# Where the pieces of the next key and value projections stand between weighing and scores, in a two-layer Perceiver kernel

## The reference, cut to what matters

```python
q, k, v = norm(x) @ Wq, context @ Wk, context @ Wv     # keys and values: 4096 x 64 per head
scores = q @ k.T * scale (+ bias)                       # 256 x 4096 per head
out = softmax(scores) @ v                               # then all heads @ Wo, added to x
```

## Time and profile before

| what | value |
|---|---|
| median of 3 runs | 2159.23 us (2150.01 to 2159.76) |
| the profiled execution, its own time | 2159.08 us |
| its span in the profile | 2157.3 us |
| busy: PE, PEld | 1940.9 us (90%), 1322.9 us (61%) |
| busy: DVE, ACT, POOL | 1633.2 (76%), 838.4 (39%), 928.3 (43%) us |
| mean granted TensorE clock | 0.941 of full speed |

### The profile page before, as it was taken

The page is one execution under the profiler, slowest core; times in us unless marked ns, Lnnn a source line. Parts: engine busy times, 40 slices in busy tenths (PEclk is TensorE's granted clock), DMA queues, the critical chain, the costliest instruction groups (busy, mean ns, idle before and its releaser), DMA issues. The chain is left out here.

```text
span 2157.3 us, 34519 instructions
## 1 busy us (share of the span) xinstructions
PE 1940.9 (90%) x12560; PEld 1322.9 (61%) x12562; DVE 1633.2 (76%) x2131; ACT 838.4 (39%) x1108; POOL 928.3 (43%) x438
## 2 busy tenths in 40 slices
PE   8999999999749889899999999999999999997526
PEld 5666666666339778656666666665666666665224
DVE  3566676667596356689988898899988999889572
ACT  3655665656330135223433334333343334334101
POOL 0354655546540034014645456454655446455200
PEclk9999999999868579999999999999999999999758
DMA  2000110000100062000000000110000000000001
GB/s 105 8 13 7 63 32 12 12 7 3 47 0 1 1 244 78 10 8 1 12 12 12 12 0 12 51 51 10 3 12 12 12 1 12 12 8 5 20 0 49
DMA packets 27717, 52.45 MB, mean 24 GB/s; under 512 B 4227, under 2 KB 15252, under 8 KB 27156
## 3 DMA queue, kind: packets, MB, share of 16 engines
q1 hardware_dynamic: 27200, 51.60, 7.4%
q10 hardware_dynamic: 468, 0.16, 0.0%
HBM read 51.23 MB, written 0.52 MB: 24 GB/s over the span
## 5 line engine op out<-in xcount | busy, mean ns | idle before, releaser
L298 POOL TENSOR_TENSOR biased_sums<-biased_sums,biased_scores 128x1024 f32<-128x1024 f32 x218 | 515.2, 2363 | 209.5 <-ACT biased_scores L524 206.1
L573 DVE TENSOR_TENSOR biased_scores<-ps,bias 128x1024 f32<-128x1024 f32 x256 | 311.1, 1215 | 79.6 <-PE ps L369 79.6
L524 ACT ACTIVATE biased_scores<-biased_scores 128x1024 f32<-128x1024 f32 x256 | 268.2, 1053 | 244.6 <-DVE biased_scores L594 243.6
L587 DVE TENSOR_TENSOR ps<-ps,biased_scores 128x512 f32<-128x512 f32 x480 | 331.9, 691 | 3.6
L594 DVE TENSOR_TENSOR biased_scores<-biased_scores,ps 128x1024 f32<-128x1024 f32 x256 | 305.0, 1211 | 11.9 <-PE ps L409 11.9
L298 POOL TENSOR_TENSOR plain_sums<-plain_sums,plain_scores 128x1024 f32<-128x1024 f32 x106 | 250.5, 2363 | 83.9 <-ACT plain_scores L524 74.9
L329 PEld LDWEIGHTS ps<-weights_again,context_again 128*128 128x128 f32 x2048 | 238.2, 192 | 70.7 <-issue 34.0
L329 PE MATMUL ps<-weights_again,context_again 128*128 128x128 f32 x2048 | 262.5, 281 | 13.5 <-ACT biased_keys L497 11.0
L320 PE MATMUL ps<-context_again,weights_again 128*128 128x512 f32 x512 | 253.0, 617 | 19.3 <-ACT biased_values L508 16.7
L369 PE MATMUL ps<-biased_queries,biased_keys 64*128 64x256 f32 x2048 | 257.4, 390 | 6.6 <-DVE biased_scores L573 5.8
L587 DVE TENSOR_TENSOR ps<-ps,plain_scores 128x512 f32<-128x512 f32 x240 | 167.4, 697 | 115.7 <-ACT plain_scores L519 111.4
(11 more groups left out here) (360 smaller groups left out, 2335.9 us busy)
## 6 DMA issues: line engine op xcount, KB each, us to landing
context<-in_ctx_t SPq DMA_DIRECT2D x8, 1024.0 KB, 5.7
moe_w<-in_moe_w SPq DMA_DIRECT2D x32, 256.0 KB, 2.8
context_again<-in_ctx_t SPq DMA_DIRECT2D x8, 1024.0 KB, 6.3
weights_again<-in_wqkv SPq DMA_DIRECT2D x45, 128.0 KB, 2.1
bias<-in_fside SPq DMA_DIRECT2D x1, 4096.0 KB, 22.6
biased_w_out<-in_w_out SPq DMA_DIRECT2D x16, 256.0 KB, 2.7
weights<-in_wqkv SPq DMA_DIRECT2D x21, 128.0 KB, 2.1
plain_w_out<-in_w_out SPq DMA_DIRECT2D x8, 256.0 KB, 2.6
```

The lines of the kernel that those rows point to most:

```text
L298: pool.tensor_tensor(both(SUM[:, :, :, :]), both((E[:, 0] if kp == 1 else SUM)[:, :, :, :]), both(E[:, kp, :, :, :]), ALU.add).then_inc(su ...
L524: act.activation(at, at, ACT.Exp).then_inc(exp_done, 1)
L573: dve.tensor_tensor(E[:, kp, :, :, :].rearrange("p (h t) n j -> p h t (n j)", h=2), scores_bank(kp).rearrange("p (h t n) -> p h t n", h=2, ...
L587: ins = dve.tensor_tensor(to, highest, E[:, kp, :, n, :], ALU.max)
```

## The change

In the two tables every group now has its piece between weighing and scores, and groups 2, 3 and 5, which have two pieces, have the second one after the scores, as they had. So V0, V1, V4, K3 and K4 move from behind the scores of groups 0, 1, 4, 6 and 7 to before them. The order of the pieces among themselves stays. The same loop on ScalarE follows; in the biased stage ScalarE's own order of instructions is the same as before, as it copies no scores there.

```diff
-BEFORE_SCORES = {2: ("V", 2), 3: ("V", 3), 5: ("V", 5)}
-AFTER_SCORES = {0: ("V", 0), 1: ("V", 1), 2: ("K", 0), 3: ("K", 1), 4: ("V", 4), 5: ("K", 2), 6: ("K", 3), 7: ("K", 4)}
+BEFORE_SCORES = {0: ("V", 0), 1: ("V", 1), 2: ("V", 2), 3: ("V", 3), 4: ("V", 4), 5: ("V", 5), 6: ("K", 3), 7: ("K", 4)}
+AFTER_SCORES = {2: ("K", 0), 3: ("K", 1), 5: ("K", 2)}
@@ TensorE
-                            if g in BEFORE_SCORES:
-                                piece(m, BEFORE_SCORES[g])
+                            piece(m, BEFORE_SCORES[g])
                             scores(m + 1, 2 * g)
                             scores(m + 1, 2 * g + 1)
-                            piece(m, AFTER_SCORES[g])
+                            if g in AFTER_SCORES:
+                                piece(m, AFTER_SCORES[g])
@@ ScalarE
-                            if g in BEFORE_SCORES:
-                                piece_out(m, BEFORE_SCORES[g])
+                            piece_out(m, BEFORE_SCORES[g])
                             if not biased:
                                 scores_out(m + 1, 2 * g, attending)
                                 scores_out(m + 1, 2 * g + 1, attending)
-                            piece_out(m, AFTER_SCORES[g])
+                            if g in AFTER_SCORES:
+                                piece_out(m, AFTER_SCORES[g])
```

## The result

The changed kernel takes 2269.8 us (median of 6 runs, 2261.8 to 2275.9), the kernel before 2152.6 us (6 runs with those shown). The ratio is 1.0534, with a 95% interval of 1.0507 to 1.0561: slower, by 117 us, where 80 were forecast and 2260 was the upper end. The profiled execution took 2270.6 us (span 2268.8), against 2159.08, so 111.5 us more; the profiled execution of the kernel before lies 6.5 us above the median of its six runs, so 111.5 and not 117 is the number to hold against the forecast of 80. Beside the first group of experiments one run of the kernel before took 8308.1 us; it is slow, and counts in no ratio.

A forecast was written before the change was run, and what follows sets the result against it. TensorE and VectorE were taken to run nearly in step, tied through ScalarE's in-order queue. Biased loop 73.4, slow loads 2, END - 2 1.8, earlier sweeps -1.4, plain loop 4.2: 80.0 us on 2159.1, so 2239 us, range 2206 to 2260.

The forecast's parts named there:

- Step 1: Sweep start: V0 waits 1.17 us for its weights and starts at 3.05; VectorE's first block comes 3.15 us later.
- Steps 2 to 5: Biased sweep: late VectorE delays K0 and K2, K4 delays the last scores; sweep grows 5.24 us to 73.8.
- step 3: Biased sweep, blocks 6 and 8: block 6 is 3.15 us late, block 8 waits 0.8; K2 starts 3.93 late.
- step 5: Biased sweep's end: V6's 0.69 us wait goes, reciprocal comes at 61.93 against 56.69; the chain behind it is unchanged.
- the clock falls: Rival: added TensorE idle time drops its clock to half, 2.4 us once in each of 14 sweeps; 2273 us, chance 0.06.
- Step 6: Other sweeps: slow first loads cost 2 us in all, biased END - 2 costs 1.8, sweeps before the loops gain 1.4.
- Step 7: Plain loop: V0 waits 1.17 us, the reciprocal comes with the last maximum; 0.7 us per sweep, 4.2 in six.
- TensorE stays the bound: Rival: V6's wait of 0.69 to 0.76 us goes in each of 20 sweeps; faster, 2144 us, chance 0.04.
- Only the load costs: Rival: load waits 1.17 us, V6 gives back 0.76; 0.4 us in 20 sweeps, 2167 us, chance 0.04.
- the load is in time: Rival: V0 starts at 1.88 without waiting, the coupling holds; 1.17 us less per loop sweep, 2214 us, chance 0.12.

The follow-up runs named there:

- order on ScalarE alone: Changed kernel, but in the biased loop ScalarE copies a group's piece out before the second exponential of the group before: 2203.4 us, 1.0229.
- The filled waits: Changed kernel with two filler matmuls before K0 and two before the peaks are spread, in the biased loop and END - 2: 2235.6 us, 1.0371.
- The last version: Kernel before with V6 writing the bank of the lowered peaks and all lowerings two blocks ahead: 2121.0 us, 0.9849.
- the version with both cures: Changed kernel with the value weights' load issued first and all VectorE lowerings two blocks ahead: 2165.7 us, 1.0056.
- the one without V0: Changed kernel with V0 back behind the scores of group 0, the other four pieces still moved: 2208.9 us, 1.0251.
- K3 and K4 alone: Kernel before with only K3 and K4 moved ahead of the scores of groups 6 and 7: 2191.9 us, 1.0171.
- the early load: Changed kernel with the value weights' load issued first in SyncE's turn, ahead of query and key weights: 2244.1 us, 1.0408.
- the two lowerings first in the changed kernel: Changed kernel with VectorE lowering blocks 4 and 5 before the first scores: 2254.0 us, 1.0464.
- V0 alone: Kernel before with only V0 of the five pieces moved before the scores: 2210.5 us, 1.0257.

## Why the prediction was wrong

The direction and the mechanism of the waits held, the size did not: 111.5 us on the profiled executions, with 80 forecast.

*Step 1.* V0's load: 3.05 forecast; in the 14 biased sweeps V0 starts at 2.77 to 3.67 us, in the first at 4.02, on the average of all 0.27 late. Near enough, and in the plain loop right on the average (3.04).

*Steps 2 to 5.* Counted from the weighing at 1192.97: block 6 at 28.13 (27.83 forecast), block 14 at 56.57 (56.26), the reciprocal at 62.24 (61.93), the spreading of the peaks at 66.91 (66.61). Each is 0.3 late by the load. This is a sweep whose clock held up to its end. The waits before K0 and K2 were 2.19 and 1.52 us (2.2 and 1.6 forecast). The order on ScalarE alone takes both away, so their cause is shown.

*The step that failed* is the pricing of TensorE's waits of 2.2 us by their own length alone. It stands in two places: in step 3, "K0 to the scores of group 3 is unchanged", behind the wait before K0, and in the last term of step 5, "7.17 us up to the next weighing", behind the wait before the peaks are spread. Both were taken at full clock, and the rival that the clock falls had 0.06 and no term in the sum. Measured, the 7.17 us are 8.86 in 10 of the 14 sweeps, and the stretch from K0 to K2 is 24.4 instead of 22.8 us in 8 of them. With one fall behind the wait of 2.07 us before V0 in the first sweep that makes 19 falls of 1.6 to 1.7 us, some 32 us, which is the excess over the forecast but for some 2 us of later loads. The filled waits show that it is the clock: the fillers leave 0.27 and 0.45 us of the two waits, no stretch is slow any more, and the loop is 33.8 us shorter. I had the price of one fall too high (2.4, measured 1.68) and its number too low (14).

*Why I ruled it out.* Step 5 has the sums wait until about 60.0 for block 15 to be copied out, which would have split the wait at the end of the sweep in two. In the code `spread_sums` waits for 15 of the 16 blocks, so for block 14, and not for the last one, as the description of TensorE above has it too; the sums are spread at 59.11 without a wait, TensorE runs on and stands still for 2.16 us in one piece before the peaks are spread. But the wait of 2.2 us before K0 was in the forecast in one piece. For it I took one idle time of 1.95 us at full speed in the sweep of END - 2 for a sign that 2.3 are harmless. The Trainium skill's rule ("TensorE: Matmul & The Clock Gate", A second HAM failure mode: psum-queue depth-cycling), told of a bf16 kernel, that frequent idle times between groups of matmuls make the clock swing, agrees with these traces: 0.96 to 0.98 over the sweeps of the changed kernel, 1.00 with the waits filled.

*Step 6.* Its parts are mostly wrong, and the rows of the table that look right are luck. The plain loop's first load was not slow (V0 waits 0.72 us), the biased loop's was (2.07). The gain of 1.4 us in the sweeps before the loops isn't there: the 0.8 us up to the plain loop come from the first load of the context, which TensorE waited for until 7.65 us before and 6.79 after, with 72.4 and 72.5 us from there on; of the 0.7 between the loops only 0.1 lies behind the first queries of the biased stage. The biased sweep of END - 2 is 1.7 us longer up to the spreading of the peaks, 1.8 forecast.

*Step 7.* Plain sweeps: 0.65 us longer on the average, 0.7 forecast. Right, with the reciprocal coming when VectorE is through.

*The rivals.* "TensorE stays the bound" falls: its gap before V6 went, and 5 us of others came. "Only the load costs" falls with K0's wait of 2.19 us, "the load is in time" with V0's waits. "The clock falls" is what came, on top of the waits; that its 2273 us lie so near the 2269.8 measured is luck, since it had 14 falls of 2.4 us where there were 19 of 1.6 to 1.7. The Trainium skill's advice to close the gaps of the most-contended engine ("Perfetto Trace Analysis", Optimization Strategy) is not refuted by the first of these. The last version closes the same gap at its source, by another bank, and gains, together with the lowerings two blocks ahead.

## What to carry to other kernels

When two engines are nearly equally loaded and tied by in-order queues, an order of work on one must be read as arrival times at the other: a consumer that comes later by one piece at its last block pays at the end of the sweep, whatever the first engine saves. Take a wait away where it arises (another bank, an earlier load, a copy that doesn't stand behind an operation that waits) before moving work across it. And where a change opens idle stretches of about two microseconds on TensorE in every round (2.07 to 2.19 us here), price the matmuls behind them at half the clock as well, 1.7 us each time here, as a case with a chance worth naming.

## What the runs showed that I had not expected

The clock falls behind waits that look alike, and not each time. Behind the wait of 2.16 us before the peaks are spread it fell in 4 of 14 sweeps in the version with both cures and in the one without V0, in 10 of 14 in the changed kernel, in 13 of 14 with K3 and K4 alone and with ScalarE's copies first, and in all 14 with the early load and with the two lowerings first in the changed kernel. Behind K0's wait of 2.19 us it fell in 8 of 14 (changed kernel) and 6 of 14 (early load). These two rows come from the version with both cures, behind three sweeps at full speed:

```profile
1288.88 1.12 PE L409 MATMUL ps<-biased_peaks_diagonal,ones 128*128 128x512 f32 x2 [2.16 <-DVE biased_peaks_diagonal L608]
1289.84 3.58 PE L417 MATMUL ps<-biased_w_out,biased_heads_out 128*128 128x256 f32 x8
```

With V0 alone, where K0's wait of 1.44 us is the longest, it never fell, and in the loops of all these versions it never fell behind a shorter wait either, up to K0's 1.65 us (28 sweeps) and one of 1.78 us before V0. What decides between two sweeps with the same waits stays open.

That VectorE can be relieved of two lowerings ahead of its first block for nothing (0.9988), while shifting all of them by two blocks is worth 16 us more than that with the same bank for V6 (2121.0 against 2137.5), was not expected either. Of the 16 us, 11 are in the biased loop (66.85 us per sweep and not 67.66); the stages between the loops, which these edits hardly touch, differ by 6 us between the two profiled executions, so the rest may be chance. My reading, not tested by itself, is that what counts is how much stands between the last scores that it waits for and the end.
